# Cross-attention kernel: each of two heads in its own 64 rows of the tensor array, a PSUM bank per head, maxima in pairs

## The reference, cut to what matters

```python
# layer 0: tokens 0..76 and 77..255 of the context are attended to apart, the results added
q = split_heads(x @ Wq.T);  k = split_heads(text @ Wk.T);  v = split_heads(text @ Wv.T)
out_text = attend(q, k, v)                     # softmax(q k^T / 4) v
out_ip   = attend(q, split_heads(ip @ Wk_ip.T), split_heads(ip @ Wv_ip.T))
x = (out_text + out_ip) @ Wo.T + bo + x
# layer 1: tokens 0..251 are text, the last 4 are image tokens
probs_t = softmax(q k_t^T * scale);  text_out = probs_t @ v_t
qsem = l2norm(probs_t @ text);       sem = qsem @ l2norm(ip).T
probs_ip = softmax(q k_ip^T * scale + 0.5 * sem) * spatial_mask
x = (text_out + probs_ip @ v_ip) @ W_out + b_out + x
```

## Time and profile before

| what | value |
|---|---|
| median of 3 runs | 886.08 us (885.2 to 886.97) |
| profiled execution, its own time | 881.61 us |
| its span | 879.8 us |
| TensorE matmuls (PE) busy | 809.0 us, 92% |
| VectorE (DVE) busy | 556.6 us, 63% |
| ScalarE (ACT) busy | 428.3 us, 49% |
| GpSimd (POOL) busy | 340.7 us, 39% |
| matmuls | 6456 |
| mean granted clock of TensorE | 0.963 |

### The profile page before, as it was taken

The page is one execution under the profiler, slowest core; times in us unless marked ns, Lnnn a source line. Parts: engine busy times, 40 slices in busy tenths (PEclk is TensorE's granted clock), DMA queues, the critical chain, the costliest instruction groups (busy, mean ns, idle before and its releaser), DMA issues.

```text
span 879.8 us, 17377 instructions
## 1 busy us (share of the span) xinstructions
PE 809.0 (92%) x6456; PEld 653.0 (74%) x6456; DVE 556.6 (63%) x1569; ACT 428.3 (49%) x922; POOL 340.7 (39%) x255
## 2 busy tenths in 40 slices
PE   5759799898989898999999999999999999989896
PEld 5758597676867677778787877877878778767575
DVE  4447254555555657576867848669678586596654
ACT  5234433535353536545545655455465554545451
POOL 6311101101010103031657547365384473665763
PEclk9889889999999999999999999999999999999799
DMA  9953922737262737374516234143053321401010
GB/s 267 245 125 103 213 85 64 189 116 184 70 173 81 186 97 190 95 197 113 140 39 162 85 85 122 58 110 121 26 139 97 86 83 58 111 1 34 1 30 16
DMA packets 102116, 96.71 MB, mean 110 GB/s; under 512 B 10152, under 2 KB 102032, under 8 KB 102032
## 3 DMA queue, kind: packets, MB, share of 16 engines
q1 hardware_dynamic: 100976, 94.61, 40.2%
q10 hardware_dynamic: 1056, 0.98, 0.4%
HBM read 57.71 MB, written 36.70 MB: 107 GB/s over the span
## 4 chain that ended last, share of the span: by engine, by line
PE 67%; DVE 9%; SPq 7%; DMA 5%; issue 5%; ACT 4%; POOL 2%; ACTq 0%; POOLq 0%; DVEq 0%
PE pB L348 19%; PE pB L464 10%; PE pB L427 7%; PE pB L450 6%; PE pB L546 5%; DMA KP<-k0d 4%; PE pPV L486 4%; PE pPV L491 3%; PE pPV L496 3%; DVE m_sb L974 3%; SPq L1294 3%; PE pPV L482 2%; PE pB L505 2%; ACT P L778 2%; POOL Y L1198 2%
## 5 line engine op out<-in xcount | busy, mean ns | idle before, releaser
L1198 POOL TENSOR_TENSOR Y<-P,wv 128x512 f32<-128x512 f32 x120 | 153.6, 1296 | 206.0 <-ACT P L778 205.9
L989 DVE TENSOR_TENSOR Y<-pB,Y 128x512 f32<-128x512 f32 x160 | 109.0, 686 | 96.0 <-PE pB L464 71.0
L427 PE MATMUL pB<-KP,QP 96*128 96x256 f32 x640 | 133.8, 292 | 25.4 <-DMA KP<-k0d 24.5
L427 PEld LDWEIGHTS pB<-KP,QP 96*128 96x128 f32 x640 | 109.1, 194 | 40.2 <-issue 18.9
L450 PE MATMUL pB<-QP,KP 100*128 100x512 f32 x320 | 114.7, 436 | 17.0 <-DMA QP<-mlo 14.2
L974 DVE TENSOR_REDUCE m_sb<-pB 128x2 f32<-128x504 f32 x160 | 108.0, 676 | 14.2 <-PE pB L427 12.4
L778 ACT ACTIVATE P<-pB 128x512 f32<-128x512 f32 x160 | 86.2, 594 | 45.9 <-PE pB L450 45.9
L1175 POOL TENSOR_TENSOR klo<-xin,khi 128x256 fp32r<-128x256 f32 x18 | 13.1, 751 | 245.5 <-ACT khi L691 245.5
L691 ACT ACTIVATE Vs<-pPV 128x512 f32<-128x512 f32 (+1 forms) x80 | 39.4, 492 | 139.0 <-PE pPV L486 106.5
L971 DVE TENSOR_REDUCE m_sb<-pB 128x2 f32<-128x154 f32 x160 | 50.0, 313 | 86.9 <-PE pB L427 86.0
L778 ACT ACTIVATE P<-pB,ln 128x512 f32<-128x512 f32 x160 | 101.3, 693 | 0.0
(11 more groups left out here) (174 smaller groups left out, 1693.7 us busy)
## 6 DMA issues: line engine op xcount, KB each, us to landing
QP<-q0d SPq DMA_DIRECT2D x64, 192.0 KB, 4.1
KP<-k0d SPq DMA_DIRECT2D x64, 192.0 KB, 4.5
c_sb<-in_cT SPq DMA_DIRECT2D x16, 512.0 KB, 4.8
q0d<-qhi SPq DMA_DIRECT2D x32, 256.0 KB, 2.5
k0d<-khi SPq DMA_DIRECT2D x30, 256.0 KB, 2.5
q0d<-qlo SPq DMA_DIRECT2D x16, 256.0 KB, 2.8
k0d<-klo SPq DMA_DIRECT2D x15, 256.0 KB, 2.7
QP<-q1d SPq DMA_DIRECT2D x32, 96.0 KB, 4.3
```

What stands on the lines that cost most here:

```text
L427: made = mm(bank[:, sc * S:sc * S + S], QP[i][0:KROWS, j, a, sc * 128:sc * 128 + 128], KP[i][0:KROWS, j, :], start=True, stop=True)
L989: tt(Y[:, p, dst, :], bank_of["gp", q, dst][:, :], Y[:, p, dst, :], MUL).then_inc(dv_y, 1)
L1198: tt(Y[:, p, ch, :], P[:, p, ch, :], PH[q % HR][ch].bitcast(F32), SUB).then_inc(po_y, 1)
```

## The change

Each head gets a half of the array's rows. Head a of a pair lies in rows 64a to 64a+47 of both `QP` and `KP`, with the four rows of the shift at 64a+48 to 64a+51. The zeros go, and `QP` has one copy instead of two. Matmuls name their place with `tile_position=(64 * a, 0)`, that is a row tile of 64 rows and 128 columns. The scores of a pair are now four matmuls of 52 rows and 256 moving columns, alternating between the two tiles, and a bank holds one head with all 256 context tokens. `maxima` makes the maxima of a pair: four matmuls of 48 rows and 256 columns, two banks. ScalarE, GpSimd and VectorE follow: an instruction has 512 elements as before, now of one head; VectorE's product waits for both differences of GpSimd.

```diff
-MAXH = (3, 3, 3, 3, 3, 3, 2, 0, 0, 0)
-MAXF = (2, 2, 2, 2, 2, 2, 2, 2, 2, 2)
+MAXH = (2, 2, 2, 1, 1, 1, 1, 0, 0, 0)
+MAXF = (1,) * 10
...
+    out += scores + weigh
     if u >= B:
-        out += scores + weigh + [("quad", q, 0)] + first + [("quad", q, 1)]
+        out += [("quad", q, 0)] + pairs[:1] + [("quad", q, 1)]
     else:
-        out += scores + first + weigh
-    out += pieces[0] + pieces[1] + rest[:1] + pieces[2] + rest[1:]
+        out += pairs[:1]
+    out += pieces[0] + pieces[1] + pairs[1:] + pieces[2]
...
-            def maximum(u, h):
-                i, j, a = u % 2, h // 2, h % 2
-                bank = take("mx", u * H + h)
...
-                    made = mm(bank[:, sc * S:sc * S + S], QP[i][0:KROWS, j, a, sc * 128:sc * 128 + 128],
-                              KP[i][0:KROWS, j, :], start=True, stop=True)
+            def maxima(u, j):
+                i = u % 2
+                banks = [take("mx", u * H + 2 * j + a) for a in range(2)]
+                pe.wait_ge(*pack_landed(u, j // 4))
+                for sc in range(2):
+                    for a in range(2):
+                        rows = slice(64 * a, 64 * a + KROWS)
+                        made = mm(banks[a][:, sc * S:sc * S + S], QP[i][rows, j, sc * 128:sc * 128 + 128],
+                                  KP[i][rows, j, :], start=True, stop=True, tile_position=(64 * a, 0))
...
+                banks = [take("sc", q, a) for a in range(2)]
                 for ch in range(2):
-                    bank = take("sc", q, ch)
-                    mm(bank[:, :], KP[i][0:QROWS, j, ch * 128:ch * 128 + 128],
-                       QP[i][0:QROWS, j, :, :].rearrange("p a s -> p (a s)"), start=True, stop=True).then_inc(pe_sc, 1)
+                    for a in range(2):
+                        rows = slice(64 * a, 64 * a + QROWS)
+                        made = mm(banks[a][:, ch * S:ch * S + S], KP[i][rows, j, ch * 128:ch * 128 + 128],
+                                  QP[i][rows, j, :], start=True, stop=True, tile_position=(64 * a, 0))
...
-            return chunk.rearrange("z (d j a) s -> (z d) j a s", a=2, d=D)
+            return chunk.rearrange("z (d a j) s -> (z d) a j s", a=2, d=D)
...
-                dma(QP[i][48 * a:48 * a + 48, js, a, :].bitcast(F32), head_rows(qd[u], m)[:, :, a, :]).then_inc(l_ld[i][m], 16)
+                dma(QP[i][64 * a:64 * a + KROWS, js, :].bitcast(F32), head_rows(qd[u], m)[:, a]).then_inc(l_ld[i][m], 16)
...
-                dv.wait_ge(po_y, 2 * k + dst + 1)
+                dv.wait_ge(po_y, 2 * k + 2)
...
-            nc.gpsimd.memset(QP[0][:, :, :, :].bitcast(F32), 0.0).then_inc(po_set, 1)
-            nc.gpsimd.memset(QP[1][:, :, :, :].bitcast(F32), 0.0).then_inc(po_set, 1)
-                        nc.gpsimd.memset(QP[(u + 1) % 2][KROWS:QROWS, :, :, :].bitcast(F32), 1e20).then_inc(po_big, 1)
...
-                    dma(QP[i][r:r + 1, :, :, :].bitcast(F32), tile[h0:h0 + H, :].bitcast(F32)).then_inc(l_m[i], 16)
+                    dma(QP[i][KROWS + r:128:64, :, :].bitcast(F32), tile[h0:h0 + H, :].bitcast(F32)).then_inc(l_m[i], 16)
...
-                    if u + 2 < U and j == NP - 1:
-                        for m in range(KC):
+                    for m in ((0, 1) if j == 8 else (2,) if j == NP - 1 else ()):
+                        if u + 2 < U:
                             load_queries(sp, dma, u + 2, m)
                             load_keys(sp, dma, u + 2, m)
```

More of the change, by code:

```diff
@@ L22 @@
 NP = H // 2
-KROWS = 96
-QROWS = 100
+KROWS = 48
+QROWS = 52
 PR = 3
@@ L88, in plan @@
     many = MAXF if u < 0 else MAXH
-    heads = [("max", u + 1, h) for h in range(sum(many[:j]), sum(many[:j + 1]))] if u + 1 < U else []
-    first, rest = heads[:1], heads[1:]
+    pairs = [("max", u + 1, p) for p in range(sum(many[:j]), sum(many[:j + 1]))] if u + 1 < U else []
     out = []
@@ L175, in build @@
         ind = sb("ind", [4, 2, S], F32R)
-        QP = [sb(f"QP{i}", [128, NP, 2, S], F32R) for i in range(2)]
+        QP = [sb(f"QP{i}", [128, NP, S], F32R) for i in range(2)]
         KP = [sb(f"KP{i}", [128, NP, S], F32R) for i in range(2)]
@@ L463, in quad @@
                 for n, (col, src) in enumerate(jobs):
-                    made = mm(bank[:, :], G[i][:, col:col + 128], ph[src], start=(n == 0), stop=(n == len(jobs) - 1))
+                    made = mm(bank[:, :], G[i][:, col:col + 128], PH[:, q % HR, src, :], start=(n == 0), stop=(n == len(jobs) - 1))
                 made.then_inc(pe_gp, 1)
@@ L604, in tensor_program @@
                         if what == "max":
-                            maximum(*a)
+                            maxima(*a)
                         elif what == "bg":
@@ L1130, in vector_program @@
                         if what == "max":
-                            maximum(*a)
+                            for h in range(2):
+                                maximum(a[0], 2 * a[1] + h)
                         elif what == "done":
@@ L1191, in weights @@
                 k, p = q - B * NP, q % PR
[L1192 to L1194 removed]
+                for a in range(2):
+                    ss = slice(S * a, S * a + S)
+                    po.wait_ge(ac_exp, 2 * q + a + 1)
+                    po.wait_ge(ac_ph, 2 * k + a + 1)
                     po.wait_ge(pe_pv, (q - PR) // 2 + 1)
@@ L1278, in load_ind @@
                 sp.wait_ge(ac_set, 2)
-                dma(KP[i][KROWS:QROWS, :, :].bitcast(F32),
-                    ind[:, L, None, :].to_broadcast([4, NP, S]).bitcast(F32)).then_inc(l_ind[u], 16)
+                for a in range(2):
+                    dma(KP[i][64 * a + KROWS:64 * a + QROWS, :, :].bitcast(F32),
+                        ind[:, L, None, :].to_broadcast([4, NP, S]).bitcast(F32)).then_inc(l_ind[u], 16)
+                    if L:
+                        sp.wait_ge(dv_set, 1)
+                        dma(QP[i][64 * a + KROWS + 2:64 * a + KROWS + 3, :, :].bitcast(F32),
+                            ones[0:2 * NP, :]).then_inc(l_ind[u], 16)
             def shift_rows(u):
@@ L1435 @@
         hm[c % 128, c // 128, c // D] = 1.0
-    order = _np.concatenate([_np.arange(128 * m, min(128 * m + 128, C)).reshape(-1, D).T.reshape(-1) for m in range(3)])
+    order = _np.concatenate([_np.arange(128 * m, min(128 * m + 128, C)).reshape(-1, 2, D).transpose(2, 1, 0).reshape(-1)
+                             for m in range(3)])
     P = lambda a: _np.ascontiguousarray(a[:, order])
```

67 lines of the change are left out of this document (26 added, 41 removed).

## The result

The changed kernel takes 896.41 us (median of 4 runs, 890.75 to 908.12), the kernel before 885.64 us beside it (4 runs, 883.2 to 886.97). The ratio is 1.0098, with an interval of 1.0063 to 1.0132. The run of 908.12, with a mean granted clock of 0.936 where the others have 0.948 to 0.954, counts as slow: it is in the median and not in the ratio. The time lies in the predicted range, but on the other side of 1: the change costs 1%, where practically no change, on the fast side, was forecast. The profiled execution took 894.36 us, 12.7 more than the one of before. That is the difference that the profile has to explain, and a few us of it are the luck of the two executions profiled.

A forecast was written before the change was run, and what follows sets the result against it. TensorE's own work (busy 809.0 of 879.8 us) and layer 0's load stalls bound it. Sum: 881.61 + 16.8 - 21.0 + 2.0 = 879.4; with the runs' median 4.5 above the profiled execution, 884 us; range 810 to 908.

The forecast's parts named there:

- TensorE's work: Both layers: fewer matmul steps save 73.6 us, changes of array shape cost 90.4; sum +16.8 us.
- Full overlap of the tiles: Scores and maxima: two row tiles work beside each other, 320 steps of 0.12 us each, together 73.6 us less.
- 0.19 us a change of shape: At each end of a run of row tiles: 476 new entries and exits at 0.19 us, 90.4 us more.
- Rivals 1, 2 and 4: Row tiles change shape for little, 806 us (0.20); half the change cost, 842 (0.15); no tile overlap, 960 (0.08).
- Layer 0's stall: Unit starts waiting for key loads: `weigh` ahead, longer scores, loads' form, head start and clock give 21.0 us less, bounds 12 and 25.
- the 3.6 us of the prediction: Layer 0: four runs of scores, each 0.16 us longer, fall into the stall at six unit starts, 3.6 us less.
- 41.5: Layer-0 units 2 to 5: a length near 41.5 us in the changed profile was named as a sign.
- 6 was put on the clock: Layer-0 units 2 to 5: the clock may stay up when the stall goes, 6 us less, at most 7.2.
- VectorE's later wait: A product waiting for both GpSimd differences delays maxima and `weigh` where TensorE has slack: 2 us more, bounds 0 and 7.
- rival 3: Layer 1, slots 0 to 2: bunched maxima put VectorE behind and TensorE waits for banks; 18 us, total 902; chance 0.15.
- The sign that the prediction named for being wrong: Slots 1 and 2: TensorE waiting for VectorE's maxima was one of three signs that the forecast is wrong.
- 16 us a unit of slack: Layer 1: VectorE's slack of 16 us a unit was the argument against the bunched-maxima rival.

The follow-up runs named there:

- e2: Changed kernel with layer 1's first pair of maxima directly behind the scores instead of between the quadratic forms: 880.46 us, ratio 0.9892 to the kernel before.
- e4: Kernel before with `weigh` ahead of the first maximum in layer 0: 867.66 us, ratio 0.9772.
- e8: Kernel before with `weigh` first in layer 0 and channels reordered so a partition's rows of a load are contiguous in DRAM: 864.33 us, ratio 0.9752.
- e9: Kernel before with `weigh` first (head start too), a third of the projections ahead of layer 0's first maximum, and whole-row key loads: 860.21 us, ratio 0.9717.
- e12: Changed kernel with all loads at the end of slot 9 again, none ahead of the shift's rows: 891.51 us, ratio 1.0101 to the kernel before.
- e10: Kernel before with only VectorE's product waiting for both differences of GpSimd: 892.16 us, ratio 1.0069.
- e5: Kernel before, full array, with maxima bunched as in the change, four heads in slots 0 to 2: 892.17 us, ratio 1.0055.
- e11: Kernel before with both VectorE's later wait and the maxima bunched four, four, four: 899.27 us, ratio 1.0163.
- e1: Changed kernel with the second pairs of maxima in slots 1, 3 and 5 instead of 0, 1 and 2: 878.31 us, ratio 0.9903 to the kernel before.
- e3: Changed kernel with both matmuls of one tile issued before those of the other, instead of alternating: 894.72 us, ratio 1.0091 to the kernel before.

## Why the prediction was right or wrong

**TensorE's work (+16.8): right in its parts.** Full overlap of the tiles: shown, two steps for four matmuls in both orders. 0.19 us a change of shape: shown, by the timeline after and by e2. The busy time of unit 11 grew by 1.4 us instead of 2.05. Its 3.0 us of idle time are all in five waits, four of them at a change of shape, so some changes may be hidden in waits; that is not shown. Rivals 1, 2 and 4 fall with this. The Trainium skill's rule that a change of mode drains the engine (TensorEngine Tiling (Array Packing), section Tiling Modes) holds in this trace for row tiles, with the 0.09 us of an entry; weights that come late cost as much again.

**Layer 0's stall (-21.0): right in its mechanism, and lucky in its sum.** With the work of the head start and layer 0, -18.5 was predicted and -19.1 measured. e4 shows that `weigh` ahead of the waiting maximum carries most of it, and with it the clock of units 2 to 5; e8 points to a smaller part of the loads. e9 comes to the same layer 0 without row tiles, so they are not needed for it; whether their longer runs of scores gave the 3.6 us of the prediction was not separated. Units 2 to 5 took 38.8 to 39.4 us, where 41.5 was named as the sign: they gave 19.7 us together, 8.5 in busy time, where 6 was put on the clock, and 11.2 in idle time. This made up for two misses. The head start was to be 0.7 us longer at most and is 4.0, because the prediction priced the issue of eight loads and not their transfers (e12); unit 0 gives 3.7 back. And unit 6 is 4.2 us longer, below.

**VectorE's later wait (+2.0, bounds 0 and 7): the step that failed.** The prediction took the low end "because most products have waited long for TensorE rather than GpSimd", and looked for slack where the kernel has it, in the last units. That is true of most products and false of the first of a unit from unit 9 on, behind which VectorE has the densest stretch of the unit. Alone it costs 6.1 us (e10), within its bounds. The bunching of the maxima stood apart, as rival 3, and was put at nothing in the sum; alone it costs 4.9 (e5). Together they cost 14.4 (e11). Put in place of the 2.0, the forecast is 884 + 12.4 = 896.4, and 896.41 is the median. That this fits to the digit is luck, since the 14.4 has an interval of 5 us. Layer 1 by itself is the better check: 14.3 for the work and 14.0 of e11 are 28.3 of the 31.8 us. So rival 3 was right in its mechanism, the bunching and the latency both, and its 18 us for them were near 14. The sign that the prediction named for being wrong, TensorE waiting for VectorE's maxima, is the wait of 0.97 us at the start of slot 1. The argument "16 us a unit of slack" was the error: VectorE has no gap in the first 13 us behind the late product, and its slack in the later slots does not help there.

In unit 11, 58.8 + 2.05 (changes) + 1.2 (wait) + 0.7 (bunching) is 62.8 of 63.0 us. But the busy time has 0.6 less than the 2.05, and e1 shows that undoing the bunching gives back 1.4, twice what it costs alone. What stands in that place is the wait of the maxima for ScalarE's bank, 0.91 us, which neither e10 nor e11 has in this unit and which is gone in e1. So pairs that take two banks at once, bunched, have a price of their own; no run has it alone.

**The clock: partly open.** It rose where a stall went, as predicted, and fell where nothing was predicted. Unit 6 of the kernel after, in four stretches:

```profile
core 0: us, PE busy (x) PEld busy (x) DVE busy (x) ACT busy (x) POOL busy (x), PEclk, DMA share, GB/s
309.10:314.10 5.00, 3.44 (x38) 2.17 (x39) 2.31 (x6) 4.84 (x11) 3.84 (x6) 1.00 0.93 226
314.10:318.00 3.90, 3.88 (x23) 3.41 (x24) 3.73 (x9) 2.16 (x5) 3.90 (x3) 0.70 1.03 223
318.00:330.00 12.00, 12.00 (x73) 8.37 (x71) 6.69 (x19) 4.23 (x8) 0.69 (x1) 0.53 0.45 135
330.00:354.00 24.00, 24.00 (x230) 19.12 (x230) 13.49 (x42) 10.65 (x23) 0.00 (x0) 1.00 0.28 85
```

After a stall of 1.55 us near the end of the first stretch the engine does 12 us of unbroken work at the lower of its two levels (1.2 GHz), 73 matmuls, and then 230 in 24 us at the full one. Unit 14 has such a stretch too. Summed over windows of 4 us, the kernel after loses 44.1 us to the clock, before 32.3, e11 41.0, e2 43.0, e9 20.9. So some 12 of the profiled 12.7 us can be booked there as well as on the waits: the two accounts overlap, since waits come ahead of the falls. What is free of the clock are the 4.3 us of each of the units 10 to 12. Ahead of the falls in units 6 and 9 TensorE waited 1.55 and 1.80 us; ahead of the one in unit 13 it waited 0.98, as in units 10 to 12, which have none. Why is open.

## What to carry to other kernels

Slack of an engine counts in the stretch where the added work or wait stands, not over a stage: an engine at 72% of a unit can be the bound in its first two slots. Put what waits for nothing ahead of what waits, which here gave 2.3% by exchanging two steps. Row tiles halve the steps of matmuls with few rows, but each run of them costs two changes of shape, 0.38 us here, which is more than three steps of 256 columns; they need long runs, or neighbours in the same shape.

## What the runs showed of the hardware

- Two row tiles overlap in either order in which their matmuls were issued (e3): with tiles in the order 0, 0, 64, 64 a run takes 0.43 us, as with 0, 64, 0, 64.
- A change between the full array and row tiles costs 0.19 us each way, about 0.09 without matmuls and 0.10 for weights that were not loaded meanwhile (timeline of the kernel after; e2, 0.38 and 0.37 for two).
- A load whose rows of a partition are one contiguous stretch in DRAM is issued in 0.45 us (e9), with separate rows in 0.63. For the queries of e9 the rows still lie apart in SBUF.
- DMAs issued behind eight loads land later even where their issue is not delayed: the scores that need them waited 8.53 us, and 4.55 without the loads (e12).
- The lower clock can last 12 us while TensorE never pauses (unit 6 of the kernel after: 12.00 of 12.00 us busy at 0.53).
